# The half-wide stage completed last, and one store moved from the build into pass 0

## What is computed

```python
edge_index = jnp.stack([src, dst])
x = _layernorm(x + _L0_gnn_ref(x, edge_index, ...))              # two sage_conv
x = _layernorm(x + _L1_gnn_ref(x, src, dst, edge_attr_16, ...))  # three message layers
...
# sage_conv: mean of x[src] over dst, times W_l, plus x times W_r
# message layer: relu(segment_sum(concat(x[dst], x[src], ea) @ W.T + b, dst)), batchnorm between them
```

## Time and profile before

| | us |
|---|---|
| median of 3 runs | 1188.8 |
| lowest and highest | 1186.09, 1193.02 |
| the profiled execution | 1187.27 |
| its span | 1185.5 |
| PE busy | 1057.4 (89%) |
| DVE busy | 732.1 (62%) |
| ScalarE busy | 344.2 (29%) |
| GpSimd busy | 104.2 (9%) |

### The profile page before, as it was taken

How to read it: one execution, slowest core, us unless ns; L and a number is a source line. 1 busy time by engine, 2 the same in 40 slices (tenths; PEclk the granted TensorE clock), 3 DMA queues, 4 the chain that set the end, 5 groups by cost and what they waited for, 6 DMA issues and landing times. The chain is left out here.

```text
span 1185.5 us, 21103 instructions
## 1 busy us (share of the span) xinstructions
PE 1057.4 (89%) x8433; PEld 658.1 (56%) x8433; DVE 732.1 (62%) x1499; ACT 344.2 (29%) x649; POOL 104.2 (9%) x125
## 2 busy tenths in 40 slices
PE   0248999999999997999999999996899998899993
PEld 0248988989999984545555444443344444344442
DVE  5798999999999853633434755444554554333444
ACT  1555556655666530200000011113310105100000
POOL 4121111222211110000000000000000000000001
PEclk9758988988898897999999999997899998899997
DMA  6334545646455348973775436745036755036750
GB/s 160 55 109 148 172 131 202 206 144 215 128 171 168 106 163 266 410 263 127 295 292 208 175 118 255 291 161 217 14 120 234 285 189 218 19 122 260 289 189 21
DMA packets 67163, 216.85 MB, mean 183 GB/s; under 512 B 32032, under 2 KB 45083, under 8 KB 53523
## 3 DMA queue, kind: packets, MB, share of 16 engines
q1 hardware_dynamic: 59044, 164.49, 39.4%
q0 software_dynamic: 8016, 50.95, 11.7%
HBM read 170.67 MB, written 44.74 MB: 182 GB/s over the span
## 5 line engine op out<-in xcount | busy, mean ns | idle before, releaser
L1293 PE MATMUL PM<-Aring,Xop 128*128 128x512 fp8e4 (+1 forms) x1960 | 398.5, 363 | 0.0
L1293 PEld LDWEIGHTS PM<-Aring,Xop 128*128 128x128 f16 x1960 | 181.5, 98 | 216.6 <-issue 16.3
L1293 PE MATMUL PM<-Ares,Xop 128*128 128x512 fp8e4 x588 | 137.6, 389 | 2.2 <-ACT Xop L1855 1.4
L1816 ACT ACTIVATE F<-PH,bag 64x512 f32<-64x512 f32 (+1 forms) x39 | 25.5, 658 | 382.4 <-PE PH L1512 382.4
L772 PE MATMUL PW<-Aring 128*128 128x52 fp8e4 (+3 forms) x2151 | 115.3, 217 | 20.3 <-ACT F L836 16.7
L772 PEld LDWEIGHTS PW<-Aring 128*128 128x128 fp8e4 x2151 | 111.5, 103 | 23.3 <-ACT F L836 18.0
L785 PE MATMUL PA<-Ares,ea 128*128 128x32 f16 x1867 | 112.3, 235 | 0.0
L1649 DVE TENSOR_SCALAR S<-PM 128x256 f32<-128x256 f32 (+1 forms) x75 | 31.4, 418 | 130.7 <-PE PM L1293 119.2
L785 PEld LDWEIGHTS PA<-Ares,ea 128*128 128x128 f16 x1867 | 108.4, 116 | 0.0
L1293 PEld LDWEIGHTS PM<-Ares,Xop 128*128 128x128 f16 x588 | 56.0, 100 | 73.1 <-issue 10.8
L836 ACT ACTIVATE F<-PW 128x392 uint16<-128x392 f32 x196 | 85.0, 506 | 6.2 <-PE PW L772 3.9
(11 more groups left out here) (149 smaller groups left out, 1113.4 us busy)
## 6 DMA issues: line engine op xcount, KB each, us to landing
Aring<-adj SPq DMA_DIRECT2D x72, 1568.0 KB, 9.8
adj<-Aring POOLq DMA_DIRECT2D x12, 1568.0 KB, 6.0
adj<-Xop POOLq DMA_DIRECT2D x12, 1568.0 KB, 6.2
Ares<-adj SPq DMA_DIRECT2D x6, 1568.0 KB, 22.3
rc<-ea_sum SPq DMA_DIRECT2D x36, 128.0 KB, 5.6
eaf<-in_erow SPq DMA_DIRECT2D x62, 51.0 KB
Aring<-adj SPq DMA_DIRECT2D x4, 784.0 KB, 4.5
rc<-rc_d SPq DMA_DIRECT2D x12, 256.0 KB, 10.3
```

Of the source, the lines that this page charges most:

```text
L1293: last = nc.tensor.matmul(o, x[:, h, :], rhs, start=h == 0, stop=h == NT - 1)
L1816: nc.scalar.activation(F[0:64, c:c + w], PH[b % 2][0:64, 0:w], ACT.Relu, bias=t["bag"][:, 4 + conv:5 + conv]).then_inc(s_hr, 1)
```

## The change

`TURN` interleaves only the banks of the full stages; the four banks of the half-wide stage 24 come last, so that stage gets rank 24 and all others move up. The store of rank 23 (`NST - 2`) is no longer issued by POOL in the build but by SP in pass 0, behind the second batch of loads and before `late_factors`, with a semaphore of its own, `s_held`, for which SP waits with the other stores. The counts for `s_st[1]` fall by one store.

```diff
--- before.py
+++ after.py
@@ -74,7 +74,7 @@
 
 BANK = 32
 BANKS = [cut(a, a + BANK) for a in range(0, NP, BANK)]
-TURN = interleaved(BANKS)
+TURN = interleaved(BANKS[0:8 * (NST - 1)]) + [*range(8 * (NST - 1), len(BANKS))]
 WINDOWS = [w for b in TURN for w in BANKS[b]]
 
 
@@ -523,7 +523,8 @@
                 if h % 2 and h // 2 + 4 < TS:
                     second(h // 2 + 4)
                 for f in unpacked_after(h) if h <= NH else []:
-                    keep(f)
+                    if f != NST - 2:
+                        keep(f)
                 for f in multiplied_after(h - 1) if h >= 1 else []:
                     keep_product(f)
                 if h >= 1 and h <= NH:
@@ -939,6 +940,7 @@
             "s_sr": [sem(f"s_sr{i}") for i in range(len(SUMS))],
             "s_rb": [sem(f"s_rb{i}") for i in range(len(FACTORS))],
             "s_fin": sem("s_fin"),
+            "s_held": sem("s_held"),
             "s_xp": [sem(f"s_xp{i}") for i in range(len(GIVEN))],
             "fl": sb("fl", [1, 16]),
 
@@ -1255,7 +1257,7 @@
                 g.sem_clear(used)
         else:
             for i in range(2):
-                g.wait_ge(m["s_st"][i], 16 * (13 - i))
+                g.wait_ge(m["s_st"][i], 16 * (13 - 2 * i))
                 g.wait_ge(m["s_eo"][i], 16 * (13 - i))
 
     @block.sync
@@ -1383,9 +1385,13 @@
             reciprocals(1)
             products(1)
             given(1)
+            st = STAGES[NST - 2]
+            n = NT * stage_width(st)
+            sp.dma_start(m["adj"][st, :, 0:n], t["Aring"][:, 1, 1, 0:n]).then_inc(t["s_held"], 16)
             late_factors()
             for i in range(2):
-                sp.wait_ge(m["s_st"][i], 16 * (13 - i))
+                sp.wait_ge(m["s_st"][i], 16 * (13 - 2 * i))
+            sp.wait_ge(t["s_held"], 16)
             sp.wait_ge(t["s_fin"], NST - EARLIER)
             reciprocals(2)
             products(2)
```

## The result

The changed kernel is slower: a median of 1200.01 us (1191.90 to 1208.31, 20 runs) against 1186.41 us (1181.27 to 1193.02, 20 runs) of the kernel before beside it, ratio 1.0109, 95% interval 1.0088 to 1.0131. The profiled execution took 1205.5 us, span 1203.7, mean granted clock 0.917 (before 1187.27, 1185.5 and 0.925). "Handover" stays SP's first issue of pass 0. It came 14.6 us later than before (458.08), and the rest of the span took 3.6 us more (745.6 against 742.0). So in this execution four fifths of the loss lie ahead of the handover, in the build, which the prediction had costed at +0.2 (and its tail at +2.0).

A forecast was written before the change was run, and what follows sets the result against it. PE was taken to bound the build, then PE and the DMA chain to meet in pass 1. There −0.4 us plus +2.0 for the clock gave +1.6, a forecast median of 1190 us, range 1182 to 1197.

The forecast's parts named there:

- Bound of the build: Build before the handover: PE, not DVE, is the limit, at 99.55 us busy of 100 against 97.23.
- rival (b): Build: DVE is the bound, so its 4.41 us wait is saved and the time is about 1183; chance 0.12.
- Build +0.2: Build up to the last ranks: a full product adds 2.7 us, a vanished PE wait takes 2.5; bounds −4.4 to +2.7.
- The clock: Start of pass 1: PE's 4.4 us idle lowers its clock for 4 us, costing +2.0 (0 to +2.8).
- Tail: Build's end: rank 24's unpack waits for rank 22's product, PE's last; handover at 445.5, +2.0 (0 to +4).
- Pass 0 on PE: After the handover: shorter late product and earlier loads let PE resume 4.2 us earlier; pass 1 starts at 512.2, not 516.3.
- The DMA chain: SP's queue, pass 0 to pass 1: the moved store's 4.0 us delays the reciprocals' write, leaving a gain of only 0.4 us.
- (a): Pass 0: the store hides under the features' load, both chains gain 4.2 us, time 1184.6; chance 0.2.
- (c): SP's wait before its third batch: the moved store holds the queue up to 10.6 us, time 1196.6; chance 0.13.

The follow-up runs named there:

- turn_only: The kernel before with only the new order of the banks, the store of rank 23 left on POOL's queue in the build; 1191.02 us, 1.0053.
- store_only: The kernel before with its old order of banks, only the store of rank 23 moved to SP in pass 0; 1189.51 us, 1.0031.
- ea_last: The changed kernel with the 808.5 KB load of attribute sums issued behind the first factors of pass 1; 1196.49 us, 1.0090 against the kernel before.

## Why the prediction was wrong

- **Bound of the build: half right.** PE bounds it in the steady part, and rival (b) fell: nothing was saved by a DVE wait that went, and handover was later than 442.
- **Build +0.2: the step that failed.** The words were that a wait of DVE counts nothing "since DVE isn't the bound". The wait that went (4.41 us) was looked up; the one that the new order makes, of rank 9 for the product of rank 7, was not, though the planner's lists for it had been worked out. It cost DVE 8.5 us. PE's idle time rose by 8.7 us, of which 4 to 5 go when the wait is taken away; the other 3.5 to 4.5 came with the new order in a way that no run singles out. Measured as the end of the build the wait is 2.7 us among the long builds (454.0 against 451.3, three traces each) and 3.8 among the short (445.4, three, against 441.7, two). Without that wait and in a short build the new order ends at 441.1 and 442.2, against my 441.9 to 442.1. That the rest of the sum came out is in part luck: these two have 4.5 us more PE idle than the kernel before, and an estimated 7 us less of the lower clock (69 against 76), which makes up for most of it.
- **The clock: mis-sized and misplaced.** I allowed the lower clock ±3 us in the range. The new order has a long build, 8.6 us longer with the wait and 9.6 without it (one and the same kernel), in 12 of 20 runs if their clock tells it. The short group's median is 1193.3, 6.9 above before; the long group's is 1204.5. By this estimate the 6.9 are about what the wait (3.8 in short builds) and the store's place (2.4 to 4.7) come to; the rest of the median's 13.6, about half of it, is the long build, and not the wait. In pass 1 the clock's term was right in kind: forecast +2.0, measured +1.7 in the profiled execution, all of it on the main product behind the post-work (12.43 against 10.74), +1.8 and, where the post-work ran at half speed too (1.97), +3.2 in the other two traces.
- **Tail: right.** The product of rank 22 is PE's last work, DVE's unpack starts 0.14 us after it ends, the handover is 3.0 us behind E (forecast 3.4).
- **Pass 0 on PE: right in kind, too good by 5 us.** PE resumes 24.6 us behind the handover, not 19.6. The second late product took 2.90. But the first took 8.07, not 7.0, and PE's idle is 7.95, not 3.6. SP's second batch did start early (5.9 us behind the handover; forecast 4.3), yet what PE waits for did not come 4.2 us sooner: the forecast had the handover-to-third-batch time without the store at 19.6 us, the runs without it have 22.6 to 23.9. An early second batch did not land as much earlier: without the store (turn_only) its last load, the features, is issued 5.2 us sooner after the handover than before (457.20 - 449.53 against 456.35 - 443.47) and takes 16.0 us to land in place of 12.8, so 2 us are gained. That it queues behind the first batch is the likely reading, but no run shows it.
- **The DMA chain: right in mechanism.** The store's 4.0 us were measured as 4.4 (28.3 against 23.9 in turn_only; 3.0 to 5.7 over the other pairs of traces); the 57.6 us from the third batch to DVE's start in pass 1 as 57.8. PE's new wait in pass 1 was forecast at 4.4 and is 4.38, but that match is partly luck: in the new order without the moved store PE waits 1.6 to 3.2 us there too, where the forecast's sums leave none, and the three traces of the changed kernel have 4.38, 4.79 and 3.33. The third batch came 28.3 behind the handover, not 23.5. From the handover to the end the forecast made 1187.1 - 445.5 = 741.6 us of the span; it is 745.6: 5.0 more up to pass 1's post-work (86.9 against 81.9), nearly all of it there by the third batch, and 1.0 less behind it.
- **Rivals.** (a) is out, the store is not hidden. (c) happened in its mechanism at about the forecast's own price, 4 us, not 10.6. It was the only rival on the slower side, and the store alone left the time within 0.5% (store_only: 1.0031). What made the kernel slower came from the build, for which no rival stood.

## What to carry to other kernels

When an order of production changes, list for every pair of stages that share a buffer how much work lies between the use and the overwrite; a pair that is one group apart can cost, also where the engine that waits is not the bound, because an engine between the two that works in the program's order (here ScalarE) carries the delay to the one that is. Put a large store behind the small write that something waits for, not ahead of it. Take a profiled execution for one sample: where a build has two lengths, compare traces (and groups of runs) of the same length and from the same chip, and see the spread of the runs before reading a difference of a few microseconds.

## What was not expected of the hardware

One kernel, with nearly the same waits of PE, has builds that differ by 9.6 us, and the difference that shows is the granted clock. The two traces come from different chips; the runs of one chip split as well. What decides it, and why the old order shows no such gap, stays open: the two traces differ from the first product on, and none of the runs tried to set it. ea_last's build fits neither (8.3 us of idle, 92 us of lower clock, E 447.8) and suggests that there are more than two. Its build is the changed kernel's, with the wait of rank 9 in it (6.4 us), and yet PE is idle no longer than in the kernel before; so the wait is not paid in full as idle time each time. Whether PE's own short stops tip the clock was not tried.
